# Scatter of a graph kernel into three partial tables instead of four, in a loop over twelve groups

## What is computed

```
neigh = segment_sum(edge_weight[:, None] * x[dst], src, 12500)    # gather at dst, add into row src
branch(v, W, b, i) = (h - mean(h)) * scale[i] / sqrt(var(h) + 1e-9) + offset[i],  h = relu(v @ W.T + b)
x1 = layernorm(x + branch(x, W_self, b_self, 0) + branch(neigh, W_neigh, b_neigh, 1))
```

## Time and profile before

| what | value |
|---|---|
| median of three runs | 5481.23 us |
| the profiled execution | 5474.58 us |
| its span, first to last instruction | 5472.8 us |
| mean granted TensorE clock | 0.719 |
| GpSimd busy | 4066.4 us, 74% |
| TensorE matmuls busy | 3514.5 us, 64% |
| VectorE busy | 2741.4 us, 50% |
| ScalarE busy | 2617.3 us, 48% |
| line 709, scatters | 1568, 2446.5 us busy |
| line 996, gathers | 1568, 1486.2 us busy |
| GpSimd's queue (q0) | 224.93 MB, 29.7% of the DMA engines' time |
| SyncE's queue (q1) | 310.47 MB, 20.3% |
| ScalarE's queue (q10) | 52.19 MB, 2.4% |

### The profile page before, as it was taken

How to read it: one execution, slowest core, us unless ns; L and a number is a source line. 1 busy time by engine, 2 the same in 40 slices (tenths; PEclk the granted TensorE clock), 3 DMA queues, 4 the chain that set the end, 5 groups by cost and what they waited for, 6 DMA issues and landing times. The chain is left out here.

```text
span 5472.8 us, 83484 instructions
## 1 busy us (share of the span) xinstructions
PE 3514.5 (64%) x18421; PEld 2921.1 (53%) x18421; DVE 2741.4 (50%) x11176; ACT 2617.3 (48%) x9201; POOL 4066.4 (74%) x3277
## 2 busy tenths in 40 slices
PE   3555555555555555555555376888888888888872
PEld 2333333443333343333433245888888888888871
DVE  4555556555655655565555384333333333333338
ACT  1222222222222222222222256888888888888863
POOL 1788888888888888888888555777777777777750
PEclk9677766666666676777676577777777777777775
DMA  7666666666666666666665783333333333333323
GB/s 257 109 111 111 119 113 111 112 112 111 112 118 113 111 112 114 113 112 117 111 112 95 144 196 101 81 79 81 82 79 81 81 79 81 81 79 81 79 74 128
DMA packets 698443, 588.07 MB, mean 107 GB/s; under 512 B 286734, under 2 KB 566184, under 8 KB 695325
## 3 DMA queue, kind: packets, MB, share of 16 engines
q0 software_dynamic: 286576, 224.93, 29.7%
q1 hardware_dynamic: 396280, 310.47, 20.3%
q10 hardware_dynamic: 15542, 52.19, 2.4%
HBM read 374.64 MB, written 212.60 MB: 107 GB/s over the span
## 5 line engine op out<-in xcount | busy, mean ns | idle before, releaser
L709 POOL DMA_INDIRECT sums_scratch<-vals,to_i x1568 | 2446.5, 1560 | 593.7 <-issue 375.0
L996 POOL DMA_INDIRECT fg<-f_scratch,src_e x1568 | 1486.2, 948 | 499.6 <-issue 477.3
L617 PE MATMUL ps_n<-same,hot 128*40 128x128 f32 x3136 | 693.9, 414 | 1349.2 <-issue 1349.2
L1049 ACT ACTIVATE hot<-raw,e_s 128x40 f32<-128x40 f32 x6272 | 1392.3, 313 | 343.7 <-DVE raw L1072 318.0
L617 PEld LDWEIGHTS ps_n<-same,hot 128*40 128x40 f32 x3136 | 557.8, 185 | 1457.9 <-issue 1394.1
L660 ACT COPY near<-ps_n 40x512 f32<-40x512 f32 x196 | 113.5, 579 | 1666.3 <-PE ps_n L617 1666.3
L1025 PE MATMUL ps_eu<-hot,prod 128*128 128x120 f32 x3136 | 891.0, 378 | 0.0
L1078 DVE TENSOR_TENSOR prod<-ps_ew,fg 128x256 f32<-128x256 f32 x392 | 164.4, 419 | 1237.8 <-DMA fg<-f_scratch,src_e 1237.8
L1023 PEld LDWEIGHTS ps_eu<-hot,prod 128*128 128x128 f32 x3136 | 623.1, 244 | 300.8 <-DVE prod L1079 213.5
L1023 PE MATMUL ps_eu<-hot,prod 128*128 128x40 f32 x3136 | 619.2, 288 | 244.5 <-DVE prod L1079 244.0
L1025 PEld LDWEIGHTS ps_eu<-hot,prod 128*128 128x128 f32 x3136 | 621.4, 246 | 0.0
(11 more groups left out here) (189 smaller groups left out, 3812.0 us busy)
## 6 DMA issues: line engine op xcount, KB each, us to landing
srow_s<-in_src SPq DMA_DIRECT2D x196, 512.0 KB
e_s<-in_edge_attr SPq DMA_DIRECT2D x196, 256.0 KB, 3.8
hid_scratch<-hid SPq DMA_DIRECT2D x196, 256.0 KB, 3.8
hid_e<-hid_scratch SPq DMA_DIRECT2D x196, 256.0 KB
sums_scratch<-zeros ACTq DMA_DIRECT2D x24, 1056.0 KB, 20.8
sums_scratch<-vals,to_i POOLq DMA_INDIRECT x1568, 3.4
fg<-f_scratch,src_e POOLq DMA_INDIRECT x1568
t_in<-sums_scratch POOLq DMA_DIRECT2D x72, 256.0 KB, 6.7
```

The source lines that it names most:

```text
L617: last = pe.matmul(ps_n[t // TH][:, t % TH, :], hot[:, k, t, :], same[:, k, t, :], start=True, stop=True)
L709: pool.indirect_dma_start(out=sums_d[i], out_offset=bass.IndirectOffsetOnAxis(ap=to_i[:, j, t:t + 1], axis=0), in_=vals[:, j, t, :], in_of ...
L996: pool.indirect_dma_start(out=fg[:, j, t, :], out_offset=None, in_=f_d, in_offset=bass.IndirectOffsetOnAxis(ap=src_s[:, j, t:t + 1], axis= ...
L1049: last = act.activation(hot[:, k, t, c, :], raw[:, k, t, :], ACT.Copy, scale=e4_s[:, j, t, c:c + 1])
```

## The change

There are three partial tables (`NTAB = 3`). The first three groups still use tables 0 and 1 in turn; from then on the n-th scatter of the stage goes to table n modulo 3, and no longer by its place in the group. How many went to a table before is counted in a list (`before_op`), and in the loop this start value is raised by 32 for each turn, that is by 12 x 8 / 3. As eight is no multiple of three, a turn of GpSimd's loop is now `TURN = 12` groups: groups 12 to 191 are 15 turns, groups 0 to 11 and 192 to 195 straight code. Setup zeroes three tables (18 transfers, not 24, by the same lines). In the node stage GpSimd adds two tables to each tile, at bodies b+1 and b+3; its multiply and add come at body b+6 instead of b+8, and SyncE loads `b_in` at b+4 instead of b+5. TensorE's wait at line 812 asks for two additions.

```diff
--- before.py
+++ after.py
@@ -44,7 +44,8 @@
 ROUND = 12582912.0
 PI = 3.14159250
 TWO_PI = (6.28125, 1.9340515136718750e-3, 1.2556635e-6)
-NTAB = 4
+NTAB = 3
+TURN = 12
 ZSPLIT = 6
 PAIRS = 3
 NPAD = 99 * P
@@ -445,7 +446,7 @@
             s_rs, s_nw, s_res = sem("self_rs"), sem("self_nw"), sem("self_res")
             sems0 = [x_ld, res_st, s_tr, s_xT, s_mm, s_relu, s_stat, s_var, s_keep, s_cen, s_hn, s_add, s_sd, s_rs, s_nw, s_res] + ld + xw_ld + added + e64_ld + hid_st + [e_tr, e_eT, e_fc1, e_sig, e_hid] + [n_srcf, n_rel, n_hot, n_same, n_before, n_away, n_away2, n_to, n_psn, n_near,
                                           n_psv, n_vals, n_scat, n_bases]
-            PER = TS // NTAB
+            assert TURN * TS % NTAB == 0 and TURN % UN == 0 and PAIRS * TS % 2 == 0
 
             npass = nc.values_load(npass_i[0:1, 0:1], min_val=1, max_val=N // W + 1)
             with nc.Fori(0, npass):
@@ -688,30 +689,40 @@
 
                     @block.gpsimd
                     def _(pool):
-                        def adds_so_far(i, s, t):
-                            if isinstance(s, int) and s < PAIRS:
-                                return s * 2 * PER + t // 2
-                            return (PAIRS * 2 * PER if i < 2 else 0) + (s - PAIRS) * PER + t // NTAB
-
-                        def body(s, q, j):
+                        ops = NSG * TS
+                        early_ops = PAIRS * TS
+
+                        def table_of(n):
+                            return n % 2 if n < early_ops else n % NTAB
+
+                        before_op = [[0] * NTAB]
+                        for n in range(ops):
+                            before_op.append([c + (i == table_of(n)) for i, c in enumerate(before_op[-1])])
+                        lo, hi = TURN, NSG // TURN * TURN
+
+                        def body(s, q, jj):
+                            j = jj % UN
                             done(pool, n_to, s)
                             done(pool, n_vals, s)
-                            pair = isinstance(s, int) and s < PAIRS
                             for t in range(TS):
-                                i = t % 2 if pair else t % NTAB
-                                if isinstance(s, int) and s in (0, PAIRS) and t < NTAB:
+                                first = s * TS + t if isinstance(s, int) else lo * TS + jj * TS + t
+                                i = table_of(first)
+                                n = before_op[first][i]
+                                if n == 0:
                                     pool.wait_ge(z_st[i], 16 * ZSPLIT)
-                                n = adds_so_far(i, s, t)
-                                if not isinstance(n, int) or n > 0:
+                                if not isinstance(s, int):
+                                    n = n + (q - lo // TURN) * (TURN * TS // NTAB)
+                                    pool.wait_ge(added[i], n * 16)
+                                elif n > 0:
                                     pool.wait_ge(added[i], n * 16)
 
                                 settle(pool, n_scat if t == TS - 1 else passed)
                                 pool.indirect_dma_start(
                                     out=sums_d[i], out_offset=bass.IndirectOffsetOnAxis(ap=to_i[:, j, t:t + 1], axis=0),
                                     in_=vals[:, j, t, :], in_offset=None, compute_op=ALU.add).then_inc(added[i], 16)
-                        sweep(pool, body, 0, NSG, 4, 192)
+                        sweep(pool, body, 0, NSG, lo, hi, TURN)
                         for i in range(NTAB):
-                            pool.wait_ge(added[i], 16 * adds_so_far(i, NSG, 0))
+                            pool.wait_ge(added[i], 16 * before_op[ops][i])
                         pool.dma_reset(range(min(x.num for x in added), max(x.num for x in added) + 1))
                 nums = sorted(x.num for x in sems0)
                 assert nums == list(range(nums[0], nums[0] + len(nums)))
@@ -770,12 +781,12 @@
                         if live(b):
                             done(sp, m_sum, b, TR)
                             sp.dma_start(flat(t_in[0:used(b), j, :, :]), rows_of(sums_d[0], b)).then_inc(t_ld[j], 16)
-                        m, r, i = at(b, q, j, 5, TR)
+                        m, r, i = at(b, q, j, 4, TR)
                         r, i = quad(r, i)
                         if live(m):
                             done(sp, m_y, m, UN)
                             sp.dma_start(flat(b_in[0:used(m), i, :, :]), rows_of(base_d, m)).then_inc(b_ld[i], 16)
-                    sweep(sp, body, 0, NB + 5, 16, 24, TR)
+                    sweep(sp, body, 0, NB + 4, 16, 24, TR)
 
                 @block.gpsimd
                 def _(pool):
@@ -788,11 +799,11 @@
                                 if t == 1:
                                     uses(pool, t_ld[i], r + 1, 16)
                                 else:
-                                    pool.wait_ge(t_acc[i], r * 48 + 16 * (t - 1))
+                                    pool.wait_ge(t_acc[i], r * 16 * (NTAB - 1) + 16 * (t - 1))
                                 settle(pool, passed)
                                 pool.dma_start(flat(t_in[0:used(m), i, :, :]), rows_of(sums_d[t], m),
                                                accum_op=ALU.add).then_inc(t_acc[i], 16)
-                        m, r, i = at(b, q, j, 8, TR)
+                        m, r, i = at(b, q, j, 6, TR)
                         r, i = quad(r, i)
                         if live(m):
                             done(pool, m_cen, m)
@@ -802,7 +813,7 @@
                             done(pool, m_hs, m)
                             uses(pool, b_ld[i], r + 1, 16)
                             pool.tensor_tensor(y[:, i % 2, :, :], y[:, i % 2, :, :], b_in[:, i, :, :], ALU.add).then_inc(m_y, 1)
-                    sweep(pool, body, 0, NB + 8, 16, 24, TR)
+                    sweep(pool, body, 0, NB + 6, 16, 24, TR)
 
                 @block.tensor
                 def _(pe):
```

## The result

The changed kernel takes 5511.2 us (median of 4 runs, 5506.8 to 5517.9), the kernel before beside it 5479.7 us: a ratio of 1.0061, 95% interval 1.0045 to 1.0077. One of the four runs of the kernel before took 11,055.8 us and is not in the ratio; without it the kernel before has 5478.2 us, 33.0 us less than the kernel after. The forecast was 5504 us. So three tables cost 0.6% here, where they save memory traffic, transfers and additions. The profiled executions are 43.3 us apart (spans 5516.1 and 5472.8 us), the medians 31.5 us: the profiled run of after is the slowest of its four, at 5517.9 us, that of before, at 5474.6 us, lies 5 us under its median.

What follows compares the result with a forecast made beforehand. GpSimd's pace was taken to bound the scatter stage, over half the span. 5474.6 + 60 - 15.7 - 21 = 5497.9 us; with the median 6.6 us above the profiled run, 5504 us, range 5465 to 5535 us (8 in 10: 5446 to 5560).

Steps and rivals of the forecast that it cites:

- Part 3: Setup: six zeroing transfers fewer on ScalarE bring the first scatter from 105.90 to about 90 us, -15.7 us.
- Part 4: Node stage: one added table fewer for each block shortens its start and its blocks, -21 us together.
- the one link: Node stage's start: one addition fewer in the chain of three into one tile, -5.5 us.
- a surplus of 21.6 us: Node stage's middle: time of 23 blocks beyond 8.71 us each; 15.5 us of it was expected to go.
- Part 2: Scatter stage: GpSimd's loop over twelve groups, in 15 turns instead of 47, saves 0, at most 15 us.
- the second rival: Scatter loop: the longer body must fetch code each turn, 51 us, giving 5530 to 5560 us; chance 0.10.
- Part 1: Scatter loop: with three tables, scatters wait for late landings, 0.31 us for each of 193 groups, +60 us.
- the third rival: Scatter loop: wait values worked out per scatter lengthen landing to start; at 1.4 us, 5630 us; chance 0.05.
- The first rival: Scatter stage: bursts cost nothing, scatter term 0 to 10 us, time 5444 to 5454 us; chance 0.18.

Runs made afterwards that it cites:

- a_zero4: The changed kernel with a fourth table zeroed in setup and never used; one run, 6489.4 us, first scatter at 105.8 us.
- b_node3: The kernel before with only the changed node stage, one of four tables left out of the sums; 6442.5 us, ratio 0.9955.
- b_turn12: The kernel before, still four tables, with GpSimd's scatter loop in turns of twelve groups; 6470.7 us against 6465.1 us, ratio 1.0006.
- tab2: The changed kernel with two tables only (NTAB = 2); 7006.3 us, ratio 1.0823 to the kernel before.
- a_pace: The changed kernel with each group's SyncE loads and store in four 256 KB parts, released by GpSimd's progress; 5457.2 us, ratio 0.9964 to the kernel before.
- b_heavy: The kernel before (four tables) with each group's 512 KB index broadcast loaded twice; one run, 5578.7 us.
- a_heavy: The changed kernel (three tables) with each group's 512 KB index broadcast loaded twice; one run, 5869.1 us.
- after_again: The changed kernel run once more, also called the repeat; 5505.6 us against 5475.5 us for the kernel before, ratio 1.0056.

## Why the prediction was right

**Part 3, zeroing: right.** -15.0 us for -15.7 us, and a_zero4 gives it back. ScalarE issues 18 transfers of zeros and SyncE's first load of the stage goes at 45.48 us, not 61.38 us; in the kernel after:

```profile
18.32 22.63 ACTq L238 DMA_DIRECT2D sums_scratch<-zeros  x18
...
45.48 0.41 SPq L464 DMA_DIRECT2D src_s<-in_src  x1
...
90.89 1.83 POOL L720 DMA_INDIRECT sums_scratch<-vals,to_i  x1 [86.14 <-ACT vals L672]
```

**Part 4, node stage: right.** -24.4 us for -21 us, and b_node3 has it alone. The start gave 5.9 us (TensorE's first tile 21.8 us after the last scatter's start, before 27.7 us) for the one link at 5.5 us; the blocks gave 17.2 us, and 1.3 us come behind them. Timeline of the kernel after, answering to the earlier trace rows:

```profile
3124.12 3.51 POOL L804 DMA_DIRECT2D t_in<-sums_scratch  x4 [5.36 <-DMA t_in<-sums_scratch]
...
3150.91 1.26 POOL L811 TENSOR_TENSOR y_m<-h_m,vecs 128x512 f32<-128x512 f32 x1 [1.81 <-DVE h_m L924]
...
3355.58 1.26 POOL L811 TENSOR_TENSOR y_m<-h_m,vecs 128x512 f32<-128x512 f32 x1 [6.09 <-DVE h_m L924]
```

From the second to the 25th block 204.7 us, 8.90 us each, before 9.65 us, for a limit of 8.71 us by VectorE. Its wait for the root falls from 20.0 us in 8 to the following, in a stretch of the same length:

```profile
DVE r_m L920 <- ACT sd_m L861: 7.2, 3, 3.4
```

These 17.2 us, of a surplus of 21.6 us, were forecast as 15.5 us.

**Part 2, the loop: right at nothing**, and the second rival falls: b_turn12, with no packet on the code queue after the loop's first turn.

**Part 1, three tables: the mechanism right, the size too small.** This is the term that was mis-sized: +60 us forecast, +79 us measured, +65 us in the repeat. What it was meant to count, the waits ended by a late landing, came to 63.5 and 52.3 us. That this is near 60 us is in part luck: I had one gap of 0.31 us in each of 193 groups, and the trace has a late landing's gap in 116 groups only, of 0.55 us a group, 34 of them with two gaps and 8 with three. The place is as forecast: the excess sits at the first scatter of a group (37.4 us) and at its last (20.8 us), just behind the loads. What the sum lacked: 13.7 us in 13 gaps (the repeat: 12.2 us) in which the scatter starts 1.5 to 2.2 us after its landing and not 0.77 us, and 3.5 us of longer instructions.

These 13 gaps follow a count of the scatters. With the scatters numbered from 0, they are at 113, 224, 335, 1001 and 1112, which is 113 and steps of 111, each with 2.1 to 2.2 us; and at 176, 234, 408, 640, 930, 1104, 1162 and 1336, which is 60 and steps of 58, each with 1.5 to 1.6 us. All of the repeat's lie on the same two rows of numbers. In tab2, where most scatters wait, both rows can be seen whole, with steps of 112 from 113 (thirteen scatters, 2.1 to 2.4 us) and of 59 from 60 (25 scatters, 1.5 to 1.9 us, and one more that comes next to the other row); of the other scatters that had to wait only one starts over 1.3 us after the landing. So with three tables the longer step is there too, and costs only where the landing is late besides. Neither 111 nor 58 is the loop's turn of 96 scatters, and tab2's scatter 60 is straight code with a constant to wait for. It is the step of the third rival, then, but not for its reason; what counts to 58 and 111 stays open.

**The first rival**, bursts that cost nothing, fell with the size above. The estimate by the Trainium skill's formula ("DMA: Bandwidth & Descriptors", section "Anatomy of one DMA") was 3.7 us from start to landing, and by it no stall. The trace of the kernel after agrees with it for the median of 3.4 us, and disagrees at the end that decides: 17% of the landings are over 4.77 us, 5% over 5.28 us. In the kernel before the share is the same, 17.6%: the late landings were there all along, hidden by the fourth table.

**The sum.** The terms give +23.3 us, the profiled executions +43.3 us: 19.2 us are missing in the scatter term and 3.6 us in the edge stage, and the node stage gave 3.4 us more than forecast. The medians are only 31.5 us apart, so the forecast is 7 us off and not 20; in the repeat the profiled span is 5498.7 us, 25.9 us over that of the kernel before, near the forecast's 23.3 us. The interval of the ratio is 0.3% wide and leaves out 1, so a change of 0.6% can be told here, well under the 2% that the prediction took as the limit.

## What to carry to other kernels

How many buffers a queue of accumulating transfers needs follows from the late landings, not from the median: the step times the number of buffers has to exceed the 95th to 99th percentile of the landing plus the time from landing to start, and the median row of a profile hides that. The runs, in us:

| run | tables x 1.85 | 95% of landings, plus 0.77 | excess |
|---|---|---|---|
| before | 7.4 | 6.0 | 3.7 |
| a_pace | 5.5 | 5.3 | 11.8 |
| after | 5.5 | 6.0 | 80.0 |
| b_heavy | 7.4 | 8.1 | 92.0 |
| a_heavy | 5.5 | 8.0 | 423 |
| tab2 | 3.7 | 5.8 | 599 |

Where it just falls short, look at what else is issued in one burst, and space that out by the consumer's own progress before adding a buffer: it gave 48 us here, more than the 31 us that the fourth table was worth in all. And a wait that is almost free before a change is read by its slack (steps times count, less landing), not by its total.

## What the runs showed of the hardware

A scatter's landing lengthens with what is issued beside it: median 3.4 us, 95% point 5.28 us with 1 MB a group in one burst, 4.54 us with the same in four pieces, 7.2 us with 1.5 MB. That the second 512 KB add 2 us to a 64 KB scatter, though it is on another queue, I had not expected.

The edge stage, untouched by any of these kernels, takes 1963 to 1966 us in before, after, after_again, a_pace, a_heavy and b_heavy, and 2907 to 2956 us on the two chips of the other runs, with the same program for that stage. In the stretch 3600 to 5000 us, first the kernel before on its own chip, then b_turn12:

```profile
3600.00:5000.00 1400.00, 1230.40 (x6975) 1148.89 (x6974) 488.80 (x1120) 1157.34 (x5169) 1059.23 (x1119) 0.76 0.32 81
```

```profile
3600.00:5000.00 1400.00, 889.87 (x4623) 806.77 (x4622) 322.94 (x740) 784.97 (x3432) 698.83 (x739) 0.68 0.21 53
```

Every engine runs a third fewer instructions, and GpSimd's waits (3500 to 5000 us of b_turn12) name SyncE's 4 KB load of indices:

```profile
POOL fg L1007 <- DMA src_e<-in_src: 496.6, 48, 14.2
```

In the kernel before, on its chip, that wait does not appear among the largest. The scatter stage is the same on both within 2 us (2937.5 and 2939.2 us). What makes it so was not tried.
